# Rotary embedding in an attention and feed-forward layer: the sine and cosine products move from SBUF to PSUM sources, the half swap moves behind the sine product, and the low half moves to GpSimd

## The reference

```
def _apply_rotary(x, cos, sin):
    d2 = x.shape[-1] // 2
    x1, x2 = (x[..., :d2], x[..., d2:])
    return jnp.concatenate([x1 * cos - x2 * sin, x2 * cos + x1 * sin], axis=-1)
q = _apply_rotary(q, cos, sin)
k = _apply_rotary(k, cos, sin)
attn = jnp.einsum('bhqd,bhkd->bhqk', q, k) * scale      # scale = HEAD_DIM ** (-0.5)
attn = jnp.where(valid, attn, neg)
attn = jax.nn.softmax(attn, axis=-1)
out = jnp.einsum('bhqk,bhkd->bhqd', attn, v)
```

## Time and profile before

| what | value |
|---|---|
| median of three runs | 394.43 us |
| span of the profiled execution | 395.7 us |
| PE busy | 361.9 us, 91% |
| DVE busy | 351.4 us, 89% |
| ACT busy | 241.6 us, 61% |
| POOL busy | 242.2 us, 61% |
| chain that ended last | DVE 38%, PE 33%, issue 15%, ACT 8%, DMA 3%, POOL 2% |

### The profile page before, as it was taken

One profiled execution on the slowest core, in us unless ns is written; L12 is line 12 of the kernel. 1 busy time (PEld: TensorE's weight loads), 2 busy tenths in 40 slices (PEclk: granted clock), 3 DMA queues, 4 the chain that ended last, 5 costly groups with the idle time before them and its releaser, 6 DMA issues.

```text
span 395.7 us, 7797 instructions
## 1 busy us (share of the span) xinstructions
PE 361.9 (91%) x2418; PEld 325.4 (82%) x2418; DVE 351.4 (89%) x672; ACT 241.6 (61%) x686; POOL 242.2 (61%) x186
## 2 busy tenths in 40 slices
PE   6978899999999999999999999999999998859697
PEld 6866788888888888888888888888888877756597
DVE  4869899999899989998999899989999999999961
ACT  2447887766676667666766776677667656417410
POOL 2327666667656665666566656665666548747960
PEclk9896999999999999999999999999999999989979
DMA  7692534233423342334233423332222220000002
GB/s 227 181 269 80 134 81 108 53 85 80 108 53 80 80 106 53 80 80 106 53 80 80 103 56 80 80 100 59 53 53 56 76 54 1 2 0 2 0 27 81
DMA packets 28129, 31.03 MB, mean 78 GB/s; under 512 B 3280, under 2 KB 19152, under 8 KB 28112
## 3 DMA queue, kind: packets, MB, share of 16 engines
q1 hardware_dynamic: 28112, 30.82, 30.2%
HBM read 12.98 MB, written 1.05 MB: 35 GB/s over the span
## 4 chain that ended last, share of the span: by engine, by line
DVE 38%; PE 33%; issue 15%; ACT 8%; DMA 3%; POOL 2%; SPq 1%; DVEq 1%; ACTq 0%; POOLq 0%
PE PR L351 7%; DVE gT_lo L784 6%; PE OT L409 6%; PE VO L369 5%; DVE rowmax L804 5%; PE SC L387 4%; DVE probsT L818 4%; DVE turn L757 4%; DVE SC L801 4%; ACT probs L600 3%; PE VO L428 3%; DVE negmax L806 2%; ACT gT_hi L610 2%; DVE xres L829 2%; DVE gT_lo L824 2%
## 5 line engine op out<-in xcount | busy, mean ns | idle before, releaser
L1024 POOL TENSOR_TENSOR turn<-turn,swapped 128x512 f32<-128x512 f32 x60 | 78.1, 1302 | 84.5 <-DVE turn L757 84.3
L1021 POOL TENSOR_TENSOR swapped<-swapped,sin_sb 128x512 f32<-128x512 f32 x60 | 79.2, 1320 | 32.3 <-DMA swapped<-turn 31.5
L409 PE MATMUL OT<-probsT,v_sb 128*128 128x128 f32 x480 | 66.7, 281 | 5.1 <-DVE probsT L818 4.9
L592 ACT ACTIVATE probs<-SC,negmax 128x128 f32<-128x128 f32 x128 | 45.9, 364 | 38.3 <-DVE negmax L806 37.8
L784 DVE TENSOR_TENSOR gT_lo<-turn,gT_hi 128x512 fp32r<-128x512 f32 x62 | 68.5, 1105 | 0.3 <-ACT gT_hi L586 0.2
L409 PEld LDWEIGHTS OT<-probsT,v_sb 128*128 128x128 f32 x480 | 59.5, 193 | 9.6 <-DVE probsT L818 9.6
L600 ACT ACTIVATE probs<-probs,rinv 128x128 f32<-128x128 f32 x128 | 44.5, 394 | 32.8 <-DVE rinv L811 32.7
L586 ACT CAST gT_hi<-turn 128x512 fp32r<-128x512 f32 x64 | 39.7, 620 | 28.6 <-POOL turn L1024 25.3
L351 PE MATMUL PR<-xT_hi,qk_lo 128*128 128x512 f32 x128 | 56.2, 439 | 0.2 <-DVE mean_abs L835 0.2
L351 PE MATMUL PR<-xT_hi,qk_hi 128*128 128x512 f32 x128 | 51.0, 398 | 0.0
L351 PE MATMUL PR<-xT_lo,qk_hi 128*128 128x512 f32 x128 | 50.6, 395 | 0.0
(11 more groups left out here) (116 smaller groups left out, 930.1 us busy)
## 6 DMA issues: line engine op xcount, KB each, us to landing
swapped<-turn SPq DMA_DIRECT2D x128, 128.0 KB, 2.3
qk_raw<-in_wq SPq DMA_DIRECT2D x16, 128.0 KB, 2.4
qk_raw<-in_wk SPq DMA_DIRECT2D x16, 128.0 KB, 2.3
v_raw<-in_wv SPq DMA_DIRECT2D x8, 256.0 KB, 2.9
o_raw<-in_wo SPq DMA_DIRECT2D x8, 256.0 KB, 2.8
xres<-in_x SPq DMA_DIRECT2D x4, 256.0 KB, 3.6
w_raw<-in_w1t SPq DMA_DIRECT2D x1, 1024.0 KB, 5.2
w_raw<-in_w2t SPq DMA_DIRECT2D x2, 512.0 KB, 3.7
```

The costliest lines, as they stand in the source:

```text
L409: last = mm(OT[:, i * P:(i + 1) * P], v_sb[:, t - 1 + b, a * HD:(a + 1) * HD], probsT[:, i, b], start=(b == b0), stop=(b == 1))
L1021: tt(swapped[c][:], swapped[c][:], sin_sb[:, half_of(c)], ALU.mult).then_inc(sin_done, 1)
L1024: tt(turn[c][:], turn[c][:], swapped[c][:], ALU.add).then_inc(rot_done, 1)
```

## The change

The sine and cosine products are both made by VectorE straight from PSUM. The sine product goes to a new tile `by_sin[c]`, and the DMA now swaps the halves of that product instead of the raw projection (the sine table is loaded with its halves exchanged to fit). GpSimd only adds, and it takes over the subtraction that makes the low part. ScalarE's copy out of PSUM is gone. The scale of the scores is multiplied into the queries' products (`scalar_tensor_tensor` for even c), so that the row maximum can be negated by the reduction itself and the small multiplication behind it goes. On ScalarE the rounding of a chunk now stands between the exponentials and the scaling, and it is one chunk younger than before (n + 3 instead of n + 2).

```
# SP
-                sp.wait_ge(proj_copied, m + 1)
+                sp.wait_ge(sin_done, m + 1)
                 for to, fr in ((0, HD // 2), (HD // 2, 0)):
                     sp.dma_start(swapped[c][to:to + HD // 2, :],
-                                 turn[c][fr:fr + HD // 2, :]).then_inc(swap_in[c], 16)
+                                 by_sin[c][fr:fr + HD // 2, :]).then_inc(swap_in[c], 16)
# PE, project(): the bank is free when the cosine product is made
-                    pe.wait_ge(proj_copied, m - 1)
+                    pe.wait_ge(cos_done, m - 1)
# ACT, pair_steps()
-                        rothi(a2, c2, m - 2)
...
-                    exps(n, j)
...
-                        copy_proj(j, m)
...
-                        scale_probs(n, j)
+                    exps(n, j)
+                    rothi(*before(s + 4, 1), n + 3)
+                    scale_probs(n, j)
# DVE
+            def times_table(dest, c, table):
+
+                hs = half_of(c)
+                if c % 2 == 0:
+                    return nc.vector.scalar_tensor_tensor(dest[:], PR[c % 2][:], SCALE, table[:, hs],
+                                                          ALU.mult, ALU.mult)
+                return tt(dest[:], PR[c % 2][:], table[:, hs], ALU.mult)
+
+            def times_sin(c, m):
+
+                dve.wait_ge(proj_done, m + 1)
+                if not (isinstance(m, int) and m < 4):
+                    dve.wait_ge(rotlo_done, m - 3)
+                times_table(by_sin[c], c, sin_sb).then_inc(sin_done, 1)
+
+            def times_cos(c):
+                times_table(turn[c], c, cos_sb).then_inc(cos_done, 1)
...
-                nc.vector.tensor_reduce(rowmax[:, j % 2], sc[:, :, 1], AX.X, ALU.max).then_inc(max_done, 1)
-                dve.wait_ge(max_done, n + 1)
-                nc.vector.tensor_scalar(negmax[:, j % 2], rowmax[:, j % 2], -SCALE, None,
-                                        ALU.mult).then_inc(negmax_done, 1)
+                nc.vector.tensor_reduce(negmax[:, j % 2], sc[:, :, 1], AX.X, ALU.max,
+                                        negate=True).then_inc(negmax_done, 1)
...
-                        rotlo(*before(s + 4, 2), m - 2)
-                        inverse_sum(n, j)
...
-                        times_cos(c1, m - 1, 2 * pair + (s + 3) // 4 + 1)
+                    times_sin(j, m)
+                    inverse_sum(n, j)
+                    times_cos(j)
# DVE, prologue
+            for c in range(2):
+                times_sin(c, c)
+                times_cos(c)
             xt_lo(0, 1)
             for c in range(2):
-                rotate_sin(c, c, 1)
-                rotate_add(c, c, cos_product[:, c * HALF:(c + 1) * HALF])
+                rotate(c, c)
             rotlo(0, 0, 0)
             rotlo(0, 1, 1)
...
+            for c in range(2, 4):
+                times_sin(c, c)
+                times_cos(c)
# POOL
                 pool.wait_ge(swap_in[c], 32 * swaps)
-                tt(swapped[c][:], swapped[c][:], sin_sb[:, half_of(c)], ALU.mult).then_inc(sin_done, 1)
                 pool.wait_ge(cos_done, m + 1)
-                pool.wait_ge(sin_done, m + 1)
                 tt(turn[c][:], turn[c][:], swapped[c][:], ALU.add).then_inc(rot_done, 1)
+
+            def rotlo(a, c, m):
+                pool.wait_ge(rothi_done, m + 1)
+                tt(rot_lo(a, c % 2)[:, half_of(c)], turn[c][:], rot_hi(a, c % 2)[:, half_of(c)].bitcast(F32),
+                   ALU.subtract).then_inc(rotlo_done, 1)
...
+                for s in range(LAST_STEPS + 1 if last else 8):
+                    m = 8 * pair + s + 3
+                    rotate((s + 3) % 4, m, 2 * pair + (s + 3) // 4 + 1)
...
+                    rotlo(*before(s + 4, 1), m)
```

More of the change, by code:

```diff
@@ L70, in preln_block_kernel @@
         turn = [sb(f"turn{c}", [P, 512]) for c in range(4)]
+        by_sin = [sb(f"by_sin{c}", [P, 512]) for c in range(4)]
         swapped = [sb(f"swapped{c}", [P, 512]) for c in range(4)]
@@ L491, in _ @@
             transpose_probs(LAST - 3, 0)
-            pe.wait_ge(proj_copied, CHUNKS)
+            pe.wait_ge(cos_done, CHUNKS)
             keep_warm(PR[1], 4)
@@ L575, in ohi @@
                 copy(o_hi[:], o_raw[:]).then_inc(ohi_done, 1)
[L577 to L581, removed]
             def rothi(a, c, m):
@@ L672, in _ @@
             rothi(0, 0, 0)
-            copy_proj(2, 2)
             rothi(0, 1, 1)
-            copy_proj(3, 3)
             copy_v(1, 1)
+            rothi(0, 2, 2)
             pair_steps(0, True, False)
@@ L753, in xt_lo, with rotate @@
                        ALU.subtract).then_inc(xt_lo_done, 1)
[L755 to L771, removed]
-                tt(swapped[c][:], swapped[c][:], sin_sb[:, half_of(c)], ALU.mult).then_inc(sin_done, 1)
-            def rotate_add(c, m, product):
-                if m > 0:
-                    dve.wait_ge(rot_done, m)
+            def times_table(dest, c, table):
[11 more added lines that the diff above has]
+                times_table(turn[c], c, cos_sb).then_inc(cos_done, 1)
+            def rotate(c, m):
+                dve.wait_ge(swap_in[c], 32)
                 dve.wait_ge(cos_done, m + 1)
-                dve.wait_ge(sin_done, m + 1)
-                tt(turn[c][:], product, swapped[c][:], ALU.add).then_inc(rot_done, 1)
+                tt(turn[c][:], turn[c][:], swapped[c][:], ALU.add).then_inc(rot_done, 1)
             def rotlo(a, c, m):
@@ L867, in pair_steps @@
                     j = s % 4
[L868 to L872, removed]
+                    merge(n, j, s < 4 and not isinstance(n, int))
                     if not (first and s == 0):
                         mask_pt(n - 1)
-                    if in_haste:
-                        times_cos(c1, m - 1, 2 * pair + (s + 3) // 4 + 1)
-                    if first and s == 0:
-                        times_cos(2, 2, 1)
-                        times_cos(3, 3, 1)
-                        inverse_sum(n, j)
-                        rotate_sin(3, 3, 1)
-                    else:
-                        if first and s == 1:
-                            dve.wait_ge(rotlo_done, 3)
-                        rotlo(*before(s + 4, 2), m - 2)
-                        inverse_sum(n, j)
-                    if not (first and s == 0) and not in_haste:
-                        times_cos(c1, m - 1, 2 * pair + (s + 3) // 4 + 1)
+                    times_sin(j, m)
+                    inverse_sum(n, j)
+                    times_cos(j)
                     if 1 <= s <= 4 and not first:
@@ L1051, in pair_steps @@
             def pair_steps(pair, first, last):
-                for s in range(LAST_STEPS if last else 8):
-                    m = 8 * pair + s + 4
-                    if first and s == 0:
-                        pool.wait_ge(rothi_done, 3)
-                        tt(rot_lo(0, 0)[:, half_of(2)], turn[2][:], rot_hi(0, 0)[:, half_of(2)].bitcast(F32),
-                           ALU.subtract).then_inc(rotlo_done, 1)
-                    if first and s == 1:
-                        pool.wait_ge(rot_done, 4)
-                    if not (first and s == 0):
-                        rotate((s - 1) % 4, m - 1, 2 * pair + (s + 3) // 4 + 1)
+                for s in range(LAST_STEPS + 1 if last else 8):
+                    m = 8 * pair + s + 3
+                    rotate((s + 3) % 4, m, 2 * pair + (s + 3) // 4 + 1)
                     if s == 1 and not last:
@@ L1077, in _ @@
             qklo(1, 1)
-            pool.wait_ge(tab_in[1], 32)
             pool.wait_ge(rot_done, 2)
             rotate(2, 2, 1)
+            pool.wait_ge(rotlo_done, 2)
+            rotlo(0, 2, 2)
             pair_steps(0, True, False)
```

42 lines of the change are left out of this document (7 added, 35 removed).

## The result

The changed kernel takes 414.99 us in the median (412.10 to 416.22), the kernel before beside it 395.48 us (394.26 to 396.85): a ratio of 1.047 (95% interval 1.043 to 1.051). It is slower by 19.5 us where 17.8 us less were forecast.

What follows compares the result with a forecast made beforehand. VectorE bounded the kernel and TensorE would next; gains of 13.8 us (loop), 2.4 (start), 0.2 (threshold steps) and 1.4 (last head) gave 17.8 us off the 394.43 us median: 376.6 us, range 370 to 388 us.

Steps and rivals of the forecast that it cites:

- What bounds the kernel before: Loop: VectorE, full from waits inside its instructions, sets the 4.99 us step, 0.34 us of it TensorE waiting.
- TensorE's floor: Loop: TensorE's own time for a full step, 4.65 us, taken as 4.70 after the change; forecast case, chance 0.67.
- VectorE's sum: Loop: VectorE drops 2.61 us and gains two PSUM products at 0.70 us each, from 4.65 to 3.4 us a step.
- The rival in which they wait for GpSimd: VectorE's products collide with GpSimd at their table reads, 1.6 us each: slower, about 402 us; chance 0.06.
- the 80% named: Sign that the forecast holds: VectorE below 80% busy in the loop of the changed kernel.
- GpSimd's sum: Loop: GpSimd keeps two operations a step, plus one more every second step: 3.2 us of 4.65.
- The chain of three steps: Loop, weighing through swap, add, rounding and scaling to a transposition: 13.6 us of 13.95, 0.35 us to spare.
- The prediction's own sign of being wrong: Loop: PE still idles ahead of its transpositions for ScalarE, which would point to the rotation chain.
- the rival beside it: Late swaps or GpSimd's low parts before an add make the rotation chain bound: 384.6 us, part to 396; chance 0.20.
- The start: First transposition at 32.9 us, 2.3 us lost; first eight steps 35.3 us instead of 40.0; net gain 2.4 us.
- The tail: Last pair: 0.2 us less in the two threshold steps, 1.4 us less up to the scores waiting for chunk 63.
- the 3.5 us that the prediction named as a sign: Sign of being wrong: swaps taking more than 3.5 us from product to GpSimd's add, where 2.9 us was taken.

Runs made afterwards that it cites:

- experiment 2: The changed kernel with ScalarE casting the weights at the start of its step, not the end, GpSimd's list untouched: 374.31 us, 0.944 of the kernel before.
- experiment 4: The kernel before with only the scale moved into the query chunks' copies and the maximum negated by the reduction, small multiplication gone: 377.24 us, 0.952.
- experiment 1: The changed kernel with the chunk's low part ahead of the weights' low part on GpSimd: 385.86 us, 0.973 of the kernel before.
- experiment 3: The changed kernel with the scaling of the probabilities ahead of the chunk's rounding on ScalarE: 389.48 us, 0.981 of the kernel before.
- experiment 8: The kernel of experiment 2 with a separate VectorE multiplication of the row maximum by -1 put back: 382.33 us, 0.967 of the kernel before.
- experiment 5: The kernel of experiment 2 with one of four casts, the output weights' at s = 6, back at its step's end: 394.51 us, 0.995.

## Why the prediction was wrong

In short: the prices of the operations were right, and a wait was left out. Without that wait the forecast of 376.6 us nearly holds, since experiment 2 takes 374.31 us. Part of that closeness is luck: by the stages of the table above its first eight steps are 2.3 us longer than forecast and its 48 steps 5.8 us shorter.

**What bounds the kernel before: right.** VectorE did, by waits inside its instructions, and TensorE's floor lay beneath: experiments 2 and 4 reach 4.58 and 4.66 us a step. The floor itself was read 0.07 us too high, since 4.65 us is a full step, and two of the eight steps weigh one block less (6 matmuls instead of 8, for the first tokens have no block before them) and take 4.41 us with the early casts.

**VectorE's sum: right.** The products read 0.67 to 0.69 us in the mean against the 0.70 taken, also beside GpSimd: the one that starts at 186.05 us in experiment 2, with GpSimd busy from 185.90 to 187.20 us, takes 0.69. The rival in which they wait for GpSimd is out. So is the surcharge for a PSUM source that the Trainium skill gives ("VectorE: DVE Perf Modes", its table of costs): 682 and 686 ns here, and in the kernel before 707 ns in the mean for the SBUF product, 0.67 us where GpSimd was idle (at 163.99 us). With the early casts, 30.40 of 40 us are 76% busy, below the 80% named.

**GpSimd's sum: the step that failed.** "GpSimd keeps two operations a step [...] With one more such operation in every second step it has 2 x 1.29 + 0.65 = 3.2 us of 4.65." I counted what GpSimd executes, not what it waits for. The weights' low part waits for a cast that stands last on ScalarE, 2.6 to 3.2 us after GpSimd asks for it in the loop. Before the change that wait was free: the adds waited for VectorE's cosine products (84.3 us in the waits of before), and by the time GpSimd got to the weights the cast was made, as in these rows of the timeline before, where it is done at 165.61 us:

```profile
164.73 1.29 POOL L1024 TENSOR_TENSOR turn<-turn,swapped 128x512 f32<-128x512 f32 x1 [1.29 <-DVE turn L757]
...
164.99 0.62 ACT L569 CAST v_hi<-v_raw 128x512 fp32r<-128x512 f32 x1
...
165.98 1.35 POOL L1012 TENSOR_TENSOR v_lo<-v_raw,v_hi 128x512 fp32r<-128x512 f32 x1
```

The change took the delay for the cosine product away, so GpSimd came early, and put the chunk's low part behind the wait. The prediction set this wait at nothing; it measured 2.6 to 3.2 us in four of eight steps, and with the rounding ahead of the scaling a pair of heads took 42.5 us instead of the 36.6 of experiment 2. Experiments 1 and 2 show it from both sides, by GpSimd's order and by ScalarE's.

**The chain of three steps: right as a mechanism, wrong in its reach.** "So the chain fits with 0.35 us to spare" agrees with experiment 2, where TensorE is busy for all of the 40 us of the loop's window. The prediction's own sign of being wrong, TensorE idle ahead of its transpositions for ScalarE, is what came: 42.5 us, 32 times. But the rival beside it had GpSimd's weights as 1.3 us of work in front of an add; with their wait it is about 4, and then the rounding ahead of the scaling hands it to TensorE (experiment 3). I let that rival end at 396 us; its price was too small by that wait. The rival that stood for a slower kernel, products that wait for GpSimd, had nothing to do with the loss.

**The start: half right.** The first transposition came at 33.9 us against 32.9 forecast and 30.6 before. The first eight steps took 44.1 us instead of 35.3: the same wait, at the same places, for 6.5 us of it. Even with early casts they take 37.6 us, so the forecast for these steps was 2.3 us too low; no run separates why. The changed kernel also had its granted clock at 0.50, the 1.2 GHz level, from 46 to 48 us, after TensorE had idled for 2.28 us up to 44.62 us, while the kernel before and experiment 2 kept 1.00 there; all three had 0.50 from 32 to 34 us, around their first transposition.

**The tail: right in sign.** The two steps with the thresholds gave 1.6 us and not 0.2, and the rest 3.6 us less than before where 1.4 were forecast. Of this, the scores that waited for chunk 63 came 10.1 us after the transposition at 341.80 us, where 10.8 were forecast and it was 12.1 before.

**The arithmetic.** Three slips that decide nothing: from 12.1 to 10.8 us is 1.3 and not 1.4; the chain of three steps adds up to 13.5 us and not 13.6; and 4.65 us a step with 2 us more at the ends gives 372 us, not 371.

## What to carry to other kernels

When an operation moves to another engine, follow the waits that already stand in that engine's list: everything placed behind a wait inherits it, and the busy share does not show it (GpSimd's was 58%). When an engine is relieved, ask which of its consumers now arrives early at a wait that used to be free. And the cheapest part of a change may be worth most: here the one removed operation alone gave 19.4 us, and everything around it, early casts included, some 3 us more, so try it alone before the rebuilding around it.

## What was not expected of the hardware

An operation on two numbers per row cost VectorE 0.76 us in the mean beside GpSimd and 0.37 us with GpSimd in another phase (experiment 8), while 0.17 us is its shortest. Its wait is set by where GpSimd stands when it starts. In experiment 8 every second one, from 70 us on, finds GpSimd idle and takes 0.17 us; the others start under GpSimd's add and end some 0.03 us after it, as at 188.87 us, which ends at 189.53 where the add ends at 189.50. In the kernel before the one at 171.72 us took 1.22 us and ended at 172.94, with GpSimd busy from 171.61 to 172.91 us. So its price is not a property of the operation alone. The merge of the first tile, which reads a mask and a constant tile in SBUF, did the same: 816 ns in the mean in the changed kernel (80 to 300 us), where it took 0.30 us with GpSimd idle (178.55 us) and 1.34 us with GpSimd busy from 200.89 to 202.18 us (201.00 us), and 300 ns with the early casts (80 to 280 us). These are the rows of their groups.

```profile
L770 DVE COPY_PREDICATED SC<-in_prev_sb,nothing 128x128 f32<-128x128 int32 x10 | 8.2, 816 | 0.3
```

```profile
L770 DVE COPY_PREDICATED SC<-in_prev_sb,nothing 128x128 f32<-128x128 int32 x11 | 3.3, 300 | 0.5
```

Open is why the first transposition varies by some 1.4 us between kernels whose lists are the same up to it, all but the casts' place in later steps: 33.9 us in the changed kernel, 33.8 in experiment 5, 32.4 in experiment 2, and 33.7 in experiment 8, which has the early casts too. The traces show where it arises, not why: from the changed kernel to experiment 2 the sine product of chunk 2 starts 0.8 us earlier (20.87 against 21.63 us), and from its end to GpSimd's add it is 5.0 us and not 5.8. Both are above the 3.5 us that the prediction named as a sign and the 2.9 us that it read in the loop, but the kernel before has 6.6 us at the same place (from 20.94 to 27.55 us), so the change did not bring it. No run was made for it.
